# A transformer layer on one core: Q/K stores as one transfer per four heads, division steps later, Wo quarters through two raw buffers

## What is computed

```python
x = x + attn(_layernorm(x), qkvw, qkvb, ow, ob)
x = x + ffn(_layernorm(x), W_gate, W_up, W_down)

# attn
qkv = x @ attn_qkvw + attn_qkvb            # then split into q, k, v and heads
scores = einsum('bhqd,bhkd->bhqk', q, k) * scale
probs = softmax(scores)
ctx = einsum('bhqk,bhkd->bhqd', probs, v)
return ctx @ attn_ow + attn_ob
# ffn
return (silu(xt @ W_gate.T) * (xt @ W_up.T)) @ W_down.T
```

## Time and profile before

| | |
|---|---|
| median of 3 runs | 3380.93 us (3376.4 to 3381.73) |
| the profiled execution, its own time | 3379.22 us |
| its span, first to last instruction | 3377.4 us |
| PE busy | 3209.0 us (95%), 14464 matmuls |
| DVE, ACT, POOL busy | 2009.3, 1453.9, 809.5 us |
| granted TensorE clock, mean | 0.980 |
| DMA packets | 160367, 332.72 MB |
| DMA engines busy with the SP queue | 32.4% |

### The profile page before, as it was taken

The page is one execution under the profiler, slowest core; times in us unless marked ns, Lnnn a source line. Parts: engine busy times, 40 slices in busy tenths (PEclk is TensorE's granted clock), DMA queues, the critical chain, the costliest instruction groups (busy, mean ns, idle before and its releaser), DMA issues.

```text
span 3377.4 us, 39237 instructions
## 1 busy us (share of the span) xinstructions
PE 3209.0 (95%) x14464; PEld 2500.5 (74%) x14464; DVE 2009.3 (59%) x3093; ACT 1453.9 (43%) x2679; POOL 809.5 (24%) x604
## 2 busy tenths in 40 slices
PE   6899999988999999999699999999999999999999
PEld 5676777766676776766377878888888788888887
DVE  5688888887888888878774432333323433323324
ACT  1377777766777777767463111111111111111111
POOL 1134333333343343423433111101011001101010
PEclk9899999999999999999799999999999999999999
DMA  3535343453443534434545631111121411111111
GB/s 103 145 103 149 98 132 105 115 149 101 114 132 90 145 87 117 129 88 126 156 135 181 201 117 38 56 57 38 40 73 44 174 56 55 40 38 63 50 49 51
DMA packets 160367, 332.72 MB, mean 99 GB/s; under 512 B 31088, under 2 KB 65008, under 8 KB 156592
## 3 DMA queue, kind: packets, MB, share of 16 engines
q1 hardware_dynamic: 160176, 330.22, 32.4%
HBM read 228.41 MB, written 101.19 MB: 98 GB/s over the span
## 4 chain that ended last, share of the span: by engine, by line
PE 80%; DVE 11%; SPq 3%; DMA 3%; ACT 2%; issue 1%; POOL 1%; ACTq 0%
PE ps L636 15%; PE ps L637 15%; PE ps L638 15%; PE ps L702 6%; PE ps L721 5%; PE ps L738 5%; PE ps L733 5%; PE ps L791 5%; PE ps L792 4%; PE ps L793 4%; DVE mx L1023 3%; DVE pl L1045 3%; SPq L1169 3%; DVE wl L995 2%; DMA cr<-r_d 1%
## 5 line engine op out<-in xcount | busy, mean ns | idle before, releaser
L1023 DVE TENSOR_REDUCE mx<-ps 128x1 f32<-128x512 f32 x1024 | 697.6, 684 | 193.3 <-PE ps L702 183.9
L860 ACT ACTIVATE pu<-ps 128x512 f32<-128x512 f32 x1024 | 616.4, 602 | 425.9 <-PE ps L721 422.1
L1123 POOL TENSOR_TENSOR pl<-pu,ph 128x512 fp32r<-128x512 f32 x320 | 436.1, 1364 | 932.3 <-ACT ph L861 932.0
L861 ACT ACTIVATE ph<-ps 128x512 fp32r<-128x512 f32 x1024 | 614.8, 600 | 0.0
L1045 DVE TENSOR_TENSOR pl<-pu,ph 128x512 fp32r<-128x512 f32 x704 | 542.5, 771 | 64.6 <-ACT ph L861 60.1
L636 PE MATMUL ps<-x2h,gh 128*128 128x512 f32 x1376 | 538.4, 391 | 10.4 <-DVE gl L1076 9.6
L637 PE MATMUL ps<-x2h,gl 128*128 128x512 f32 x1376 | 537.9, 391 | 0.0
L638 PE MATMUL ps<-x2l,gh 128*128 128x512 f32 x1376 | 537.4, 391 | 0.0
L1085 DVE TENSOR_TENSOR hf<-ps,sg 128x512 f32<-128x512 f32 (+1 forms) x88 | 60.9, 692 | 708.6 <-PE ps L638 700.0
L702 PE MATMUL ps<-kst,qst 96*128 96x512 f32 x1024 | 425.5, 416 | 46.2 <-DVE mx L1023 34.9
L738 PE MATMUL ps<-pl,vt 128*65 128x512 f32 x1024 | 411.5, 402 | 29.8 <-POOL pl L1123 29.8
(11 more groups left out here) (91 smaller groups left out, 4625.8 us busy)
## 6 DMA issues: line engine op xcount, KB each, us to landing
wraw<-in_wqkv SPq DMA_DIRECT2D x24, 1024.0 KB, 5.5
q_d<-stg SPq DMA_DIRECT2D x384, 64.0 KB, 1.7
k_d<-stg SPq DMA_DIRECT2D x384, 64.0 KB, 1.7
qst<-q_d SPq DMA_DIRECT2D x64, 384.0 KB, 3.9
kst<-k_d SPq DMA_DIRECT2D x64, 384.0 KB, 4.7
graw<-in_wg SPq DMA_DIRECT2D x44, 512.0 KB, 4.7
graw<-in_wu SPq DMA_DIRECT2D x42, 512.0 KB, 3.5
draw<-in_wd SPq DMA_DIRECT2D x42, 512.0 KB, 3.9
```

Source lines behind the costliest of these rows:

```text
L860: e.activation(pu[sl][:, :], bk[:, :], ACT.Exp, scale=SCALE).then_inc(s["a_p"], 1)
L861: e.activation(ph[sl][:, :], bk[:, :], ACT.Exp, scale=SCALE).then_inc(s["a_ph"], 1)
L1023: e.reduce_max(mx[:, j % 2, t, half:half + 1], ps[2 + bank_of["a", j, t, half]][:, :], AX.X).then_inc(s["v_mx"], 1)
L1123: e.tensor_tensor(pl[sl][:, :], pu[sl][:, :], ph[sl][:, :], ALU.subtract).then_inc(s["g_pl"], 1)
```

## The change

Only the order of steps and the shape of transfers change; every matmul stays.

- Q/K stores get a step of their own, `qkst`, 2 calls behind `ql`. Each of the three parts is one transfer with the destination `q_d[4c:4c+4, rows, columns]` (4 heads x 32 rows x 512) out of 128 partitions of `stg`: 3 transfers of 256 KB for 12 of 64 KB.
- `mrow`'s two transfers become a step `mst`, one call later. `u`'s stores become `ust`, 2 calls later, and the two to `c_d` become one of 2 x 32 x 1024. `r_d` is stored in a step `rst`. The four `cr<-r_d` become one whose source repeats each head's row 32 times (4 x 32 x 512).
- `cdiv` stands 14 calls behind `cin` (6 for the last chunk), `ch` 5 for 4, `cst` 3 for 2; the second half's `cin` comes 40 and not 30 calls after the chunk's start.
- Wo: `oraw` becomes two buffers (the second where `bo_b` is), so a quarter can load while the one before is split; the bias load waits until Wo is split; the loads of `xr` and `ct` are spread by `defer`, and `xbo` stands further behind. The first output tile's sum waits for the bias.
- `nload` of the second batch element is deferred by 4 to 8 calls for 1 to 2.
- `gin` is SP's part of `gload`. The third unit's load is issued ahead of the `yin` loads, the first units of the second batch element earlier, and its `yin` loads move behind the first gate/up group.

```diff
@@ -59,11 +59,16 @@
     follow["qh"] = lambda c, what, half: [(1, ("ql", c, what, half))]
+    follow["ql"] = lambda c, what, half: [(2, ("qkst", c, what, half))]
+    follow["mrow"] = lambda j: [(1, ("mst", j))]
+    follow["zinv"] = lambda c: [(2, ("rst", c))]
+    follow["oload"] = lambda i: [(6 + n, ("ohi", i, n)) for n in range(4)]
+    follow["boload"] = lambda: [(8, ("xbo", 0)), (11, ("xbo", 1))]
     follow["ohi"] = lambda i, n: [(2, ("olo", i, n))]
-    follow["cin"] = lambda c, half: [(5, ("cdiv", c, half))]
-    follow["cdiv"] = lambda c, half: [(4, ("ch", c, half))]
+    follow["cin"] = lambda c, half: [(14 if c < B * KT - 1 else 6, ("cdiv", c, half))]
+    follow["cdiv"] = lambda c, half: [(5, ("ch", c, half))]
     follow["ch"] = lambda c, half: [(2, ("cl", c, half))]
-    follow["cl"] = lambda c, half: [(2, ("cst", c, half))]
+    follow["cl"] = lambda c, half: [(3, ("cst", c, half))]
@@ -151,8 +156,8 @@
     def second_batch():
-        defer(1, "nload", 1, 2)
-        defer(1, "nload", 1, 3)
+        defer(7, "nload", 1, 2)
+        defer(8, "nload", 1, 3)
@@ -162,53 +167,62 @@
                 if t + 4 < TT:
-                    defer(2, "nload", 1, t + 4)
+                    defer(4, "nload", 1, t + 4)
...

-    def split_o(i):
+    def split_o(i, units):
         for n in range(4):
-            defer(1 + n if i == 0 else 4 + n, "ohi", i, n)
+            defer(units + n, "ohi", i, n)
...
         if b == 0:
-            split_o(0)
-            while ("ql", B * KT - 1, 1, 1) not in made:
+            split_o(0, 1)
+            while ("qkst", B * KT - 1, 1, 1) not in made:
                 yield None
-            step("boload")
-            for n in range(2):
-                step("ctload", n)
-                step("xrload", n)
-                defer(5, "xbo", n)
-            for i in range(1, 4):
-                while ("olo", i - 1, 3) not in made:
-                    yield None
-                step("oload", i)
-                split_o(i)
-                while i == 1 and ("olo", 1, 3) not in made:
-                    yield None
+            defer(3, "oload", 1)
+            defer(6, "xrload", 0)
+            defer(8, "ctload", 0)
+            defer(16, "xrload", 1)
+            defer(18, "ctload", 1)
+            while ("olo", 0, 3) not in made:
+                yield None
+            defer(3, "oload", 2)
+            while ("olo", 1, 3) not in made:
+                yield None
+            defer(3, "oload", 3)
...
                     yield None
+                if n == 0 and half == 1:
+                    defer(3, "boload")
...
                         groups.append(("osum", n, half))
-                        defer(2, "osum", n, half)
+                        if n:
+                            defer(2, "osum", n, half)
                     yield 3
-                if half == 0 and n + 2 < B * TT:
+                if n == 0 and half == 1:
+                    while ("xbo", 0) not in made:
+                        yield None
+                    step("osum", 0, 0)
+                    defer(1, "osum", 0, 1)
+                if n == 0 and half == 0:
+                    continue
+                if half == (n == 0) and n + 2 < B * TT:
...
                         yield None
-                    if n:
-                        until("ystore", n - 1)
-                    step("ctload", n + 2)
-                    step("xrload", n + 2)
-                    defer(6, "xbo", n + 2)
+                    while n and ("ystore", n - 1) not in made:
+                        yield None
+                    defer(2, "ctload", n + 2)
+                    defer(3, "xrload", n + 2)
+                    defer(12, "xbo", n + 2)
@@ -220,8 +234,10 @@
                         defer(1, "nload", 2, t + 2)
-                if t in (4, 5):
-                    step("gload", t - 4)
+                if t in (3, 4):
+                    step("gin", t - 3)
+                if t in (5, 6):
+                    step("gload", t - 5)
@@ -244,7 +260,7 @@
                 for half in range(2):
-                    until("ql", j // 4, what, half)
+                    until("qkst", j // 4, what, half)
@@ -274,7 +290,7 @@
         for half in range(2):
-            until("ql", 0, what, half)
+            until("qkst", 0, what, half)
@@ -325,10 +341,13 @@
             step("u", j, half)
-            if half == 1 and j % 4 == 3:
-                sums.append(j // 4)
+            if half == 1:
+                defer(2, "ust", j)
+                if j % 4 == 3:
+                    sums.append(j // 4)
     def inverse(c):
+        until("ust", 4 * c + 3)
@@ -345,14 +364,13 @@
             inverse(c)
-            parts += [(u + 10, c, 0), (u + 30, c, 1)]
+            parts += [(u + 9, c, 0), (u + 40, c, 1)]
...
             _, c, h = parts.pop(0)
-            until("zinv", c)
-            step("cin", c, h)
-            defer(5, "cdiv", c, h)
+            until("rst", c)
+            defer(1, "cin", c, h)
         if t == 0:
-            until("mrow", j)
+            until("mst", j)
@@ -374,12 +392,14 @@
     for h in range(2):
-        defer(12 + h, "cin", c, h)
+        defer(13 + h, "cin", c, h)
...
     transposed(2, TT - 1)
+    step("gin", 2)
+    step("gload", 2)
@@ -392,6 +412,7 @@
         if i < B * NGU:
+            step("gin", i)
@@ -404,11 +425,9 @@
             gate_up(b, f)
-            if f == 0:
-                load_gu(base + 2)
-                if b == 0:
-                    step("dload", 0, 0)
-                    step("dload", 0, 1)
+            if f == 0 and b == 0:
+                step("dload", 0, 0)
+                step("dload", 0, 1)
@@ -416,6 +435,11 @@
                     load_gu(base + 2 * f + 4)
+                elif b == 0:
+                    step("gin", NGU + 1)
+            if b and f == 0:
+                for t in range(TT):
+                    step("yin", 1, t)
@@ -443,9 +467,8 @@
         if b == 0:
-            load_gu(NGU + 1)
-            for t in range(TT):
-                step("yin", 1, t)
+            step("gload", NGU + 1)
+            load_gu(NGU + 2)
@@ -1061,7 +1084,7 @@
                     dve.wait_ge("g_oh", i * 4 + n + 1)
-                    e.tensor_tensor(xl[:, k, z], oraw[:, k, :], xh[:, k, z], ALU.subtract).then_inc(s["v_ol"], 1)
+                    e.tensor_tensor(xl[:, k, z], oraw[i % 2][:, k, :], xh[:, k, z], ALU.subtract).then_inc(s["v_ol"], 1)
@@ -1126,7 +1149,7 @@
                     i = int(n == 2 * B * KT)
-                    pool.wait_ge(f"d_c{i}", 96 if i else 96 * n)
+                    pool.wait_ge(f"d_c{i}", 48 if i else 48 * n)
@@ -1134,10 +1157,10 @@
                     k, z = slice(2 * n, 2 * n + 2), slice(256 * i, 256 * i + 256)
-                    pool.wait_ge("d_o", 16 * (i + 1))
+                    pool.wait_ge(f"d_o{i % 2}", 16 * (i // 2 + 1))
...
                     pool.wait_ge("p_v", of_v(B * NG - 1, TT - 1))
-                    e.tensor_scalar(xh[:, k, z], oraw[:, k, :], 1.0, 0.0, ALU.mult, ALU.add).then_inc(s["g_oh"], 1)
+                    e.tensor_scalar(xh[:, k, z], oraw[i % 2][:, k, :], 1.0, 0.0, ALU.mult, ALU.add).then_inc(s["g_oh"], 1)
@@ -1187,7 +1210,7 @@
                         elif t < 4:
-                            sp.wait_ge(f"d_stg{t % 2}", 192 * (of_qk(KT - 1, 1, 1) // 2))
+                            sp.wait_ge(f"d_stg{t % 2}", 48 * (of_qk(KT - 1, 1, 1) // 2))
@@ -1215,47 +1238,44 @@

-                elif what == "ql":
+                elif what == "qkst":
...
                     for r, part in enumerate(three):
-                        for h in range(4):
-                            copy(dst[4 * c + h, HD * r:HD * r + HD, halves(half)], stg[sl][HD * h:HD * h + HD, part, :], f"d_stg{sl}")
+                        copy(dst[4 * c:4 * c + 4, HD * r:HD * r + HD, halves(half)], stg[sl][:, part, :], f"d_stg{sl}")
...
                     m = of_qk(j // 4, 1, 1)
-                    sp.wait_ge("d_stg0", 192 * (m // 2))
-                    sp.wait_ge("d_stg1", 192 * (m // 2))
+                    sp.wait_ge("d_stg0", 48 * (m // 2))
+                    sp.wait_ge("d_stg1", 48 * (m // 2))
...

-                elif what == "mrow":
+                elif what == "mst":
...

-                elif what == "u":
-                    j, half = at_
-                    if half == 1:
-                        sp.wait_ge("a_u", 2 * (j + 1))
-                        copy(c_d[0, HD * j:HD * j + HD, :], uu[j % 2][0:HD, :], f"d_u{j % 2}")
-                        copy(c_d[1, HD * j:HD * j + HD, :], uu[j % 2][HD:2 * HD, :], f"d_u{j % 2}")
-                        copy(z_d[j:j + 1, :], uu[j % 2][64:65, :], f"d_u{j % 2}")
+                elif what == "ust":
+                    j, = at_
+                    sp.wait_ge("a_u", 2 * (j + 1))
+                    copy(c_d[:, HD * j:HD * j + HD, :], uu[j % 2][0:2 * HD, :], f"d_u{j % 2}")
+                    copy(z_d[j:j + 1, :], uu[j % 2][64:65, :], f"d_u{j % 2}")
...
                     for i in range(2):
```

(35 more changed lines are left out.)

## The result

The changed kernel takes 3509.65 us (median of 4 runs, 3504.63 to 3515.64) beside 3381.31 us of the kernel before (3376.40 to 3381.73): 1.0384 times as long (1.0363 to 1.0404), 128 us more. The forecast was slower, 3440 us, 59 us more. Direction and range held, but the size was less than half of what was measured.

A forecast was written before the change was run, and what follows sets the result against it. PE's own work, its idle time and the lower clock were taken to bound the kernel. The profiled 3379.2 us, less 55 saved, plus 115 added by crowded engines, gave 3439, about 3440 us; range 3305 to 3545.

The forecast's parts named there:

- Few engines: Outermost count limits a transfer's DMA engines: merged Q/K stores and cr run on 4, merged c_d stores on 2.
- saturated: Rival, chance 0.08: at 16 GB/s per engine a backlog grows and attention runs at two engines' pace, 3600 us or more.
- The start: First chunk: its four Q/K sets drain later, 11 us, and the next sets delay head 0's maxima, 8: +28 us.
- The maxima and what else stands in attention: In attention the maxima's transfers queue behind merged stores; PE waits 7 us per eight heads, 56 in all: +84 us.
- the factor for the clock: Each us of PE's idle time in attention counts 1.5, since idle time also costs 0.4 to 0.8 us in clock.
- The last division: End of attention: z_d store behind c_d on one engine, cdiv 4 calls later, little projection left to cover: +3 us.
- The division: Division on POOL: moving cdiv further behind cin removes 16.6 us of PE's waits for POOL, -25 us.
- Gate and up: Feed-forward: loads issued ahead of yin remove the waits for gl, 9.6 us in three places, -14 us.
- The projection stage: Start of projection: deferring xbo removes a 13.2 us PE wait, -20, less 4 for a later first output tile: -16 us.
- The missing filler: Start of projection: for 13 calls PE has no filler work and waits for DVE's maxima, 4 us (bounds 0 and 10).
- Spread: Rival, chance 0.15: the merged transfers run on all 16 engines, nothing is added, 3311 us (3290 to 3335).
- Covered: Rival, chance 0.17: 4 and 2 engines, but mst mostly meets an empty queue; startup 20, maxima 15: 3362 us (3340 to 3390).

The follow-up runs named there:

- e1_all_split: The changed kernel with its new order of steps, but every merged transfer (Q/K, c_d, cr) taken apart again as before the change: 3341.77 us.
- e12_zin_later: The changed kernel with zinv 14 calls behind zin for 6, cin 8 calls later (not chunks 14 and 15), and zin itself 7 calls later: 3506.2 us.
- e2_qk_split: The changed kernel with only the Q/K stores taken apart (12 for 3), c_d and cr still merged: 3384.04 us.
- e5_cd_split: The changed kernel with only the c_d stores taken apart (2 for 1), Q/K and cr still merged: 3432.59 us.
- e7_division_only: The kernel before with only POOL's division moved: cdiv 14 calls behind cin for 5, second half's cin after 40 calls for 30: 3355.31 us.
- e8_nload_earlier: The new order, c_d and cr apart, 3 interleaved Q/K stores a set; second batch element's input loads deferred 5, 6, 2 calls for 7, 8, 4: 3322.92 us.
- e4_interleaved: The changed kernel with c_d and cr apart and Q/K weight columns interleaved over heads, so 3 stores a set have outermost count 32: 3331.4 us.

## Why the prediction came out as it did

**Few engines: right.** That 4 and 2 engines would be used came out of a count of completions in the trace, and the count after is 4 a store. The Trainium skill's rule ("DMA: Bandwidth & Descriptors", section "Why a DMA increments its semaphore by 16 and not by 1") agrees in each case that the runs show: an outermost count of 32 gives 16 completions a store, 4 gives 4, and 2 gives 2. The advice of the same page of the Trainium skill to coalesce many small transfers (section "Rules for kernel authors") holds only beside that rule: 3 stores for 12 cost 90 us with an outermost count of 4 and gained 10 with one of 32 (3331.4 against 3341.8).

**The rate: right.** 23 GB/s per engine was taken and 25 measured. The first four sets were to drain until 109.4 us, and the first stack was issued at 109.67. The range's other end, 16 GB/s, and with it "saturated", was not met. (9.4 MB at 23 GB/s are 410 us and not the 430 of the text, which changes its share of 0.85 by 0.01.)

**The start: near.** +28 was forecast, as 19 us of PE's idle time times 1.5. Against e1_all_split, which has the same order, the start is 149.8 - 132.5 = 17 us longer, with 55.0 us of idle time (length less busy time) for 39.7. So the idle time was near, 15 us, and each us cost 1.1.

**The maxima and what else stands in attention: the step that failed.** +84 was forecast, from 56 us of idle time times 1.5. Against e1_all_split attention is 1794.7 - 1642.1 = 153 us longer. PE's idle time there is 199.4 against 88.3 us, 111 us more, and each has cost 1.4. So the factor for the clock was right in this stage, and the idle time was sized at half. Three waits make up nearly all of it. The maxima took 85.6 us in 19 waits (2.4 us in e1_all_split), for the 56 in 14. The stacks behind the first chunk took 16.9 us (1.9), priced at nothing ("10 us to spare"). DVE's own maxima, not priced at all, took 46.5 us for 35.7.

The prediction had looked at one head as it lies in the trace of before and moved only the ends of its stores. It held SP's issue times fixed, whereas in the run SP stands 288 us for unlanded stores where it stood 40. The text had noticed `zin` ("5 us for 2 now") and left it within the bounds; it is 9.1 us a time, for 2.2. How much of the doubled idle time comes from SP's standing is not shown: e12_zin_later puts a price of 25 us on 117 us of it, without being faster than the changed kernel, and e2_qk_split has 127.2 us of it in `zin` at a cost of 42 us in all. What is shown is that the text added the two stores' bytes per engine but priced no interaction: 36 us exist only with both merged.

**The last division:** +3 forecast, 142.0 - 131.4 = 10.6 measured. About 8 of it are the merged `c_d` with the row of sums behind it: the stage takes 133.9 us in e1_all_split, and 143.5 in e2_qk_split, where `c_d` is merged and Q/K is not, but 136.5 in e5_cd_split.

Crowding in all costs 3509.65 - 3341.77 = 168 us for the 115 forecast.

**The savings: 38 for 55.** The division gave 24 for 25, but the number met by luck in part. In e7_division_only PE's wait for POOL fell by 20.1 us and not by 16.6, its wait for the maxima rose by 8.2, and 7 us of the 24 lie in heads 56 to 63, where the text had counted them to the start of the projection. Gate and up gave 1443.1 - 1427.3 = 15.8 for 14, right.

The projection stage was forecast at 16. From head 56 to 63 it went from 218.2 us before to 208.9 in e1_all_split, so 9 (before in two windows, then e1_all_split):

```profile
1565.80:1699.60 133.80, 101.66 (x369) 67.17 (x368) 99.37 (x144) 74.08 (x141) 53.98 (x43) 0.82 0.49 142
1699.60:1784.00 84.40, 82.94 (x358) 61.80 (x357) 68.09 (x106) 55.24 (x104) 33.30 (x22) 1.00 0.50 147
```

```profile
1546.90:1657.00 110.10, 95.59 (x364) 63.92 (x363) 92.31 (x142) 72.34 (x141) 46.41 (x40) 0.89 0.53 157
1657.00:1755.80 98.80, 89.16 (x365) 65.27 (x364) 74.47 (x110) 55.61 (x106) 37.87 (x24) 0.93 0.50 144
```

The idle time fell by 9.5 us (33.6 to 24.1), near the 10.5 that the text has (13.2 less 4 / 1.5), but each us gave 1.0 and not 1.5: the clock is higher in the first window and lower in the second. The missing filler did not make the wait for DVE's maxima dearer (12.4 us before, 7.8 after); the catching up that follows has a wait of 7.4 us for the first output tiles' sum instead.

The later `nload`s were costed at nothing and cost 8 us: the stage from head 24 to 28 takes 134.0 us in e1_all_split and 125.6 before, and e8_nload_earlier gives them back. What limits there is how early the input tiles come, and the text had named no cover for them.

```profile
723.50:857.50 134.00, 109.69 (x538) 80.32 (x536) 104.28 (x162) 81.41 (x162) 40.54 (x32) 0.92 0.29 91
```

```profile
731.30:856.90 125.60, 107.10 (x537) 80.12 (x536) 101.17 (x163) 82.42 (x162) 40.16 (x32) 0.93 0.34 98
```

These are e1_all_split and before. PE's busy time differs by 2.6 us and its idle time by 5.8.

**The rivals.** "Spread" is out for this change, but e4_interleaved realised it at 3331 us by another layout. "Covered" is out: it gave the maxima 15 us. Only with the Q/K stores apart (e2_qk_split, 13.8 us for the maxima) did the crowding cost no more than the order saved.

## What to carry to other kernels

Before merging transfers, write down the outermost count of both sides: a store of 4 heads x 32 rows runs on four engines, and reordering the layout so that the 32 comes first keeps both the few issues and all 16 engines. When a store gets slower, ask not only which load waits in line behind it, but which wait on the issuing engine is for that store, and do not hold the issue times of the old trace fixed: SP stood 288 us here for 40. Price two crowding edits on one resource together, since the second costs more once the first is there.

## What was not expected of the hardware

A DMA engine moves 2 KB rows at 24 to 25 GB/s whether 2, 4 or 16 work: 50, 100 and 380 GB/s in the three windows above. SP is held at the issue itself when few engines have much to do. An issue of a merged Q/K store takes 0.56 us by the median but up to 5.3, where the same 256 KB over 16 engines take at most 1.3. The rows give the shortest, median and longest issue in ns, for the kernel after and for e4_interleaved:

```profile
L1192 SPq DMA_DIRECT2D k_d<-stg x96: 503/555/5302, 88.1 to 1756.8; - x96
```

```profile
L1192 SPq DMA_DIRECT2D k_d<-stg x96: 518/602/1295, 85.3 to 1581.7; - x96
```

So 3 issues for 12 do not always free SP. In one place of the kernel after three of them took 7.03 us:

```profile
1011.35 7.03 SPq L1192 DMA_DIRECT2D q_d<-stg  x3
```
